# One position of FFN2 computed plainly instead of with 7 quarter products, and other hands for the last block's adds and stores

## What is computed

```python
def quant_linear(x, w, b):
    xq, s_in = quant_act_uint8(x)              # one scale for the whole tensor, 0..255
    wq, s_w = quant_weight_int8_perchannel(w)
    bq = quant_bias_int32(b, s_in, s_w)
    return jnp.einsum('btd,fd->btf', xq, wq) + bq
h = jax.nn.relu(quant_linear(x, w1, b1))       # FFN1: 512 -> 2048
return quant_linear(h, w2, b2)                 # FFN2: 2048 -> 512
x = x + _L0_ffn_ref(_L0_cond_ref(cond_512, cond_512, x, L0_cond_W, L0_cond_b), ...)
```

## Time and profile before

| what | value |
|---|---|
| median of 3 runs | 324.08 us (324.06 to 324.85) |
| the profiled execution: its own time | 324.02 us |
| its span | 322.2 us |
| PE, DVE, ACT, POOL busy over the span | 96%, 87%, 65%, 38% |
| granted clock of PE, mean | 0.999 of full |
| FFN2, from its first product at 208.46 us | 113.7 us of the span |

### The profile page before, as it was taken

How to read it: one execution, slowest core, us unless ns; L and a number is a source line. 1 busy time by engine, 2 the same in 40 slices (tenths; PEclk the granted TensorE clock), 3 DMA queues, 4 the chain that set the end, 5 groups by cost and what they waited for, 6 DMA issues and landing times.

```text
span 322.2 us, 4978 instructions
## 1 busy us (share of the span) xinstructions
PE 308.4 (96%) x1715; PEld 200.5 (62%) x1715; DVE 281.9 (87%) x622; ACT 209.6 (65%) x386; POOL 122.9 (38%) x101
## 2 busy tenths in 40 slices
PE   7999999999999999999999999999999999979793
PEld 6868888888686444444444444444478468768582
DVE  1698989997977699999999999899998689999986
ACT  2435785588377994566666663199869959878520
POOL 1076525634450699990370002341403200235342
PEclk9999999999999999999999999999999999999999
DMA  6999999999973397996990260342999978986137
GB/s 224 202 241 235 226 215 233 260 221 371 281 164 65 69 278 42 380 421 263 420 380 3 51 213 0 121 142 69 409 364 412 417 288 300 413 332 215 48 130 260
DMA packets 51912, 75.57 MB, mean 235 GB/s; under 512 B 20376, under 2 KB 35504, under 8 KB 47152
## 3 DMA queue, kind: packets, MB, share of 16 engines
q1 hardware_dynamic: 51696, 74.99, 77.7%
q10 hardware_dynamic: 192, 0.28, 0.3%
HBM read 45.89 MB, written 25.17 MB: 221 GB/s over the span
## 4 chain that ended last, share of the span: by engine, by line
PE 76%; DVE 13%; issue 4%; DMA 3%; SPq 2%; ACT 2%; DVEq 0%; ACTq 0%
PE bank L635 24%; PE bank L760 20%; PE bank L862 13%; PE bank L873 8%; PE bank L732 6%; DMA x_in<-in_x_dram 3%; DVE bank L1439 3%; DVE hidden L1262 2%; PE bank L747 2%; DVE hidden L1123 1%; DVE hidden L1417 1%; ACT w_t L1085 1%; DVE hidden L1423 1%; DVE bank L1449 1%; SPq L361 1%
## 5 line engine op out<-in xcount | busy, mean ns | idle before, releaser
L1262 DVE TENSOR_SCALAR_CACHE_REDUCE hidden<-bank,qb,hmax 128x512 f32<-128x512 f32 x62 | 47.4, 809 | 6.2 <-PE bank L760 3.8
L533 POOL TENSOR_TENSOR x_lo<-hidden,x_hi 128x512 fp32r<-128x512 f32 x28 | 35.4, 1296 | 45.7 <-ACT x_hi L953 45.7
L635 PE MATMUL bank<-x_hi,cw_hi 128*128 128x512 f32 x128 | 48.4, 394 | 0.8 <-DVE hidden L1128 0.6
L635 PE MATMUL bank<-x_lo,cw_hi 128*128 128x512 f32 x128 | 48.4, 390 | 0.0
L635 PE MATMUL bank<-x_hi,cw_lo 128*128 128x512 f32 x128 | 48.4, 389 | 0.0
L1282 DVE CUSTOM_DVE_ANT_0 hidden<-hidden,bank,hmax 128x512 f32<-128x512 f32 x66 | 45.9, 743 | 0.2
L616 POOL TENSOR_TENSOR pool_r<-pool_r,steps 128x512 f32<-128x512 f32 x16 | 20.6, 1299 | 66.3 <-DVE hidden L1425 37.4
L1085 ACT ACTIVATE w_t<-hidden,s_quant 128x512 uint8<-128x512 f32 x56 | 36.4, 721 | 9.8 <-PE bank L862 7.8
L1085 ACT ACTIVATE pool_q<-hidden,s_quant 128x512 uint8<-128x512 f32 x63 | 39.6, 712 | 0.4 <-PE bank L873 0.3
L760 PE MATMUL bank<-pool_r,pool_q 128*128 128x512 f16 x144 | 36.3, 379 | 0.0
L961 ACT ACTIVATE pool_r<-pool_q,winv 128x512 int8<-128x512 f32 x28 | 17.9, 711 | 21.6 <-DVE winv L1146 21.6
(11 more groups left out here) (170 smaller groups left out, 558.0 us busy)
## 6 DMA issues: line engine op xcount, KB each, us to landing
hidden_spill<-hidden SPq DMA_DIRECT2D x16, 1024.0 KB, 10.0
hidden<-hidden_spill SPq DMA_DIRECT2D x16, 1024.0 KB, 12.4
x_in<-in_x_dram SPq DMA_DIRECT2D x32, 256.0 KB, 7.1
pool_r<-in_x_dram SPq DMA_DIRECT2D x8, 1024.0 KB, 5.8
pool_q<-in_L_ffn_w_dram SPq DMA_DIRECT2D x7, 1024.0 KB, 10.2
out_dram<-pool_r SPq DMA_DIRECT2D x7, 1024.0 KB, 9.6
pool_r<-in_L_cond_W_dram SPq DMA_DIRECT2D x2, 1024.0 KB, 10.2
x_in<-in_L_ffn_w_dram SPq DMA_DIRECT2D x1, 1024.0 KB, 5.5
```

The costliest lines, as they stand in the source:

```text
L533: pool.tensor_tensor(x_lo[:, n % 2, k, :], x_t[:, k, :], x_hi[:, n % 2, k, :].bitcast(F32), ALU.subtract).then_inc(lo_ready, 1)
L635: return pe.matmul(REL[ot][:, :], w[:, k, ot * P:(ot + 1) * P], v[:, n % 2, k, :], start=(k == 0 and w is cw_hi and v is x_hi), stop=(k == ...
L1262: dve.tensor_scalar(hidden[:, at:at + TB], y_bank[:, :], qb1[:, ft:ft + 1], hmax[:, ft:ft + 1], ALU.add, ALU.max, accum_out=hmax[:, ft:ft ...
```

## The change

Position 5 leaves FOLDED, so that PLAIN is (0, 1, 3, 5) and FOLDED is (2, 4, 6, 7). In position 7 POOL adds all of row 0 and the last halves of rows 1, 2 and 3, which DVE now scales into OUT_ROWS as in other positions; DVE goes on adding the first halves of rows 1, 2 and 3 itself. SP stores position 6 in four DMAs of a row each (256 KB), position 7 in a DMA for row 0, three for the last halves (128 KB each) and three for the first halves.

```diff
-        FOLDED = (2, 4, 5, 6, 7)
+        FOLDED = (2, 4, 6, 7)
...
         BY_POOL = (0,) + FOLDED
         ROWS = {n: (0, 1, 2, 3) for n in BY_POOL}
-        ROWS[NB - 1] = (0,)
...
-        LAST_PIECES = [("m12b", 1, LAST), ("m22a", 2, LAST), ("m22b", 3, LAST), ("m11b", 1, FIRST),
-                       ("m21a", 2, FIRST), ("m21b", 3, FIRST)]
+        LAST_PIECES = [("m11b", 1, FIRST), ("m21a", 2, FIRST), ("m21b", 3, FIRST)]
+        LAST_TAKES = ("m12a", "m12b", "m22a", "m22b")
...
-            for n in range(SLOTS, NB - 1):
+            def store_part(n, j, cols):
+                at = n % SLOTS * WC + j * D
+                sp.dma_start(out_blocks[(n + SLOTS) % NB, :, j, cols], x_res[:, at + cols.start:at + cols.stop]
+                             ).then_inc(stored[n % 2], 16)
+
+            for n in range(SLOTS, NB - 2):
                 store(n)
-            def store_last(j, cols):
...
-            for j in ROWS[NB - 1]:
-                sp.wait_ge(summed, rows_to(NB - 1, j))
-                store_last(j, slice(0, D))
-            for name, j, cols in LAST_PIECES:
-                sp.wait_ge(last_added, LAST_PIECES.index((name, j, cols)) + 1)
-                store_last(j, cols)
-            sp.wait_ge(stored[0], 16 * SLOTS)
-            sp.wait_ge(stored[1], 16 * (SLOTS - 1 + len(ROWS[NB - 1]) + len(LAST_PIECES)))
+            for n in (NB - 2, NB - 1):
+                for j in ROWS[n]:
+                    sp.wait_ge(summed, rows_to(n, j))
+                    store_part(n, j, LAST if n == NB - 1 and j > 0 else slice(0, D))
+            for i, (_, j, cols) in enumerate(LAST_PIECES):
+                sp.wait_ge(last_added, i + 1)
+                store_part(NB - 1, j, cols)
+            sp.wait_ge(stored[0], 16 * (SLOTS - 1 + TJ))
+            sp.wait_ge(stored[1], 16 * (SLOTS - 1 + TJ + len(LAST_PIECES)))
...
                     xs = x_res[:, n % SLOTS * WC + j * D:n % SLOTS * WC + (j + 1) * D]
+                    if n == NB - 1:
+                        cols = LAST if j > 0 else slice(0, D)
+                        pool.wait_ge(fold_taken, takes_to(n, LAST_TAKES[r]))
+                        pool.tensor_tensor(xs[:, cols], xs[:, cols], OUT_ROWS[n % 2][:, j, cols], ALU.add
+                                           ).then_inc(summed, 1)
+                        continue
...
             def scale_row(n, row, cols, r):
-                if n == NB - 1 and row not in ROWS[n]:
+                if n == NB - 1 and row > 0 and cols == FIRST:
```

More of the change, by code:

```diff
@@ L499, in _ @@
             reuse(3)
-            for n in range(SLOTS, NB - 1):
-                store(n)
-            def store_last(j, cols):
-                sp.dma_start(out_blocks[SLOTS - 1, :, j, cols],
-                             x_res[:, (SLOTS - 1) * WC + j * D + cols.start:(SLOTS - 1) * WC + j * D + cols.stop]
-                             ).then_inc(stored[1], 16)
-            for j in ROWS[NB - 1]:
-                sp.wait_ge(summed, rows_to(NB - 1, j))
-                store_last(j, slice(0, D))
-            for name, j, cols in LAST_PIECES:
-                sp.wait_ge(last_added, LAST_PIECES.index((name, j, cols)) + 1)
-                store_last(j, cols)
-            sp.wait_ge(stored[0], 16 * SLOTS)
-            sp.wait_ge(stored[1], 16 * (SLOTS - 1 + len(ROWS[NB - 1]) + len(LAST_PIECES)))
+            def store_part(n, j, cols):
[3 more added lines that the diff above has]
+            for n in range(SLOTS, NB - 2):
+                store(n)
+            for n in (NB - 2, NB - 1):
[7 more added lines that the diff above has]
+            sp.wait_ge(stored[1], 16 * (SLOTS - 1 + TJ + len(LAST_PIECES)))
         @block.gpsimd
```

## The result

The changed kernel takes **319.82 us** (median of 4 runs, 319.69 to 320.28), the kernel before 324.07 beside it: a ratio of 0.9862, 95% interval 0.9843 to 0.9882. The profiled execution took 319.93 us with a span of 318.1. Predicted were 319.9 and a span of 317.99. In the changed kernel most lines stand eight further down: L873 is now L881, L1439 is L1447, and so on.

What follows compares the result with a forecast made beforehand. PE was taken to lead, with DVE the bound in positions 5 and 6 and the end a third stage. A gain of 4.21 us, 3.16 from position 5 plain and 1.05 from the end, gave 319.9 us, range 319.1 to 321.9.

Steps and rivals of the forecast that it cites:

- Part 1: Positions 4 to 7, with position 5 plain: 51.75 us instead of 54.91, so position 7 starts 3.16 us sooner.
- There DVE is the bound: Positions 5 and 6: DVE busy for 13.59 and 13.97 us, PE for only 12.6 in each.
- Part of why: DVE late in positions 5 and 6: partly its own price, L1420 taking 1.65 us beside POOL's adds, 0.69 alone.
- The cover of the reload: Before position 7: its reload's last quarter lands 3.0 us before ACT begins its tiles, so late data costs nothing.
- Part 2: End, position 7: POOL adds the last halves at 0.72 us each, so DVE ends 1.18 us sooner.
- Rival B: End: POOL's half rows cost 1.27 us each and hold up the end; time 321.5, chance 0.12.
- Part 3: Stores at the end: SP is the last link, last issue at 315.72, span ends 2.27 us later at 317.99.
- A: Seams stay: positions 4, 6 and 7 keep their times, only 5 changes; gain 0.64 us, time 322.4, chance 0.10.
- D: End: the cut-up stores run one after another, each landing before the next; slower, time 328.8, chance 0.03.
- C: A and B together: gain 0.1 us, time 324.0, no change; chance 0.03.

Runs made afterwards that it cites:

- the run with POOL later: Kernel before, but where two folded positions follow, POOL adds rows 1 and 2 only after three of the next-but-one position's first four sums: 321.43 us.
- the run with ACT's stores: Changed kernel, but the three first halves of position 7 are stored from ACT's queue instead of SP's: 319.35 us.
- the run of position 5 alone: Kernel before with position 5 plain as the only change, last block's pieces and stores as before: 321.02 us, ratio 0.9893.
- the run with one large store: Changed kernel, but position 6 is stored as one DMA of 1 MB behind its fourth row: 321.06 us.
- early 2a: Changed kernel, but a folded position behind a folded one starts its first product when m11a is taken, not m11b: 319.33 us.

## Why the prediction was right

- **Part 1, the positions.** 3.16 us forecast, 3.17 measured (54.91 - 51.74), each position on its own within 0.01. Every case after the change had its like in the trace of before, and a position's length depended only on what stood ahead of it and behind it. The run with position 6 plain shows that for a third arrangement, in three positions to 0.01; its position 5, which had no like, took 12.23 where 12.4 was expected.
- **Why PE waited there.** The prediction says "There DVE is the bound", and calls POOL beside the sums "Part of why". That is too weak: the run with POOL later took both inner waits away, 2.6 us, and left DVE its 27 operations in each of positions 5 and 6. With a plain position 5 the sums of position 6 are made while POOL is idle (POOL's adds end at 277.77, the sums begin at 280.40). By the 2.8 us of that run this is the larger part of what the plain position brings. The size came out right because position 4, from which position 6 was priced, has no contention either: its sums take 0.68 to 0.69 us. For position 6 the prediction did not check this, so its 13.30 was a good likeness and some luck.
- **The cover of the reload** held: ACT began position 7 when PE was done with position 5, at 288.62.
- **Part 2.** DVE's end 1.18 us nearer to PE's: measured 2.41 before and 1.24 after, 1.17. The half row of POOL, priced from two sizes of another type, 0.72: measured 0.72 to 0.73. Rival B is out.
- **Part 3.** SP as the last link, as the run with ACT's stores shows. The last issue was put 14.23 us after position 7's start and came at 14.09; the issue behind POOL's last half row came 0.38 after it, where the pitch was taken as 0.49.
- **Rivals.** A's 0.64 us is refuted by the run of position 5 alone, D by the time itself and by the run with one large store, and C falls with A and B. The sum, 4.21, came out as 4.1 on the spans and 4.34 on the yardstick. That the span came within 0.11 us of the forecast is partly luck: position 4 started 0.24 us later than in the kernel before, and the end was 0.13 better than forecast. Of the seam, the one wait that the prediction left in place, the early 2a then took 0.56.

## What to carry to other kernels

Price a rearranged stage by finding, for each piece, one in the trace with the same neighbours ahead and behind; that gave four positions to 0.01 us. Before a cheaper form of the arithmetic is given up because an engine is late, look whether its operations are longer there than elsewhere: here a wait on POOL was worth 2.8 us with nothing recomputed. At the end of a kernel store in pieces as they are ready, keep large transfers out of the queue (0.75 us here), and issue the last ones from an engine that is free (0.46 us).

## What the runs showed of the hardware

- A float16 operation of two SBUF operands on DVE, 128x1024, takes 0.69 us alone. Beside POOL's adds it takes 0.90 to 1.81, by how the two overlap, and most often 1.64 to 1.65; POOL's 1.27 becomes up to 1.81. A DVE operation of 128x256 with one operand in PSUM stays at 0.42 to 0.43 beside the same adds. The Trainium skill, SBUF — State Buffer (SBUF: two separate sides) says that the two engines share a pair of ports, and that a DVE instruction with two SBUF inputs and a POOL instruction each hold it to their end. The trace agrees: 1.65 is 0.69 and 0.96 more, most of a POOL add of 1.27.
- An issue of a small store by SP takes 0.33 us when the one before began 0.67 us or more ahead of it, and 0.45 right behind another (pitch 0.49). Behind a store of 1 MB the first takes 0.34, and the second and third 0.90 to 1.25 us.
- The start of position 4 moves by up to 1.9 us between executions of the same work (261.78 to 263.63). Below half a per cent a stretch of the trace tells more here than a few runs' medians.
